# A graph network kernel: weighted one-hot windows and one weight difference made by GpSimd instead of VectorE

## The chip, the cores and the metric

One Trainium2 chip, one core. The metric is the device time of the kernel in microseconds (us), the median of several executions; less is better. A profile is one further execution with the hardware profiler on; its times are counted from the start of its span.

## The reference

The inputs are 625 nodes with 256 features, 10625 edges in order of their destination (`src`, `dst`), a weight for each edge, and the weight matrices. Cut to what matters:

```python
def edge_conv(x, src, dst, W, b):
    m = concat([x[dst], x[src] - x[dst]]) @ W + b
    return segment_sum(m, dst, 625) / maximum(count(dst), 1)

h = relu(layernorm(x));  xs = [h]
for W, b in ((W0, b0), (W1, b1), (W2, b2)):
    h = relu(edge_conv(h, src, dst, W, b));  xs.append(h)
x = x + concat(xs) @ Wf + bf
h = relu(layernorm(x))
agg = segment_sum(edge_weight * (h @ W4)[dst], src)
x = x + relu(batchnorm(agg + bias) * gamma + beta)
```

Since `[x_i, x_j - x_i] @ [Wa; Wb]` is `x_i @ (Wa - Wb) + x_j @ Wb`, each layer has own terms with the difference of the two halves of its weights, and neighbour terms that a matrix of edge counts sums up.

## The kernel before, in words

The edges are never gathered. The kernel builds two dense 625x625 matrices, the edge counts and the summed edge weights, and then works with matrix products alone.

**The build.** The edges are cut into 85 tiles of 125. Tile t gives a one-hot of its sources (`src_hot`, 125 edges by 626 nodes in f16), and a narrow one-hot of its destinations: as the edges are sorted by destination, those of a tile fall into a window of 28 nodes. Windows are made for a class of 17 tiles at once (`PER` = 17, classes 0 to 4). `plain_window(c)` (L569 to 572) compares the window's ids with the edges' destinations and writes `dst_hot[:, c, 0]`, 125x504 f16. `weighted_window(c)` (L574 to 579) multiplies that by the high and the low part of the edge weights and writes `dst_hot[:, c, 1:3]`, 125x1008 f16. TensorE multiplies source one-hot by the three kinds of destination one-hot (L1276, 505 products), block of 125 destinations by block (r = 0 to 4). Block 0 takes tiles 0 to 18 and block 1 tiles 15 to 35, each for five column groups s; from block 1 on, the tiles of a block come in two halves, and only the first column group of a half waits for tiles that are new.

**Who makes what.** VectorE makes the source tiles in order (L583, `source_tile`), one `tensor_scalar` each, 77 of the 85. ScalarE makes eight of them (`SCALAR_TILES`) by two activations each. The order of VectorE's other work in the build is written out by hand in a loop over t (from L622): at tile 13 the vectors, at the last tile but one of each class (t % 17 == 15) the next class's plain and weighted window, at tiles 30, 38 and 42 the low part of u (L596), which wait for ScalarE's high part and so for TensorE, at tile 33 `difference(0)` (L586 to 590), which subtracts the halves of layer 0's weights in `raw[0]` in place, and at tile 62 the test of the flag. There are 36 slots for source tiles (`RING`): tile t waits until TensorE has finished with tile t - 36.

**What waits for it.** Before the first tile of a class TensorE waits for that class's weighted window (`weighted_windows_ready`, L1264 to 1265). Between the blocks it does other work: within block 0 the transposes of h and the neighbour terms of blocks 0 and 1, behind it those of the other blocks (L1189), and behind block 1 layer 0's own terms (L1200, `own_terms_0`, which waits for `w_diff`). SP reloads `raw[0]` once the own terms are done.

**GpSimd** makes constants in the first 4 us. Then it waits for all 77 source tiles of VectorE (`pool.wait_ge(src_hot_vector, 77)`), sums parts of the weights (L487) and makes low parts of weight matrices (L481) in the later stages.

**Behind the build** come the three layers. VectorE forms the reciprocals of the counts (L659, L661) right behind its last source tile, and then for each quarter of a layer `pre = sum * inv_count` (L742, the sum in PSUM) and `pre = pre + own` (L746, all in SBUF).

Of the kernel before, what the change touches and what calls it, by code (L numbers as in the profile page):

```python
# [34 lines left out]
ALU = mybir.AluOpType  # L35
# [7 lines left out]
KF = D // P  # L43
LAYERS = 3
NB = 5
BLK = NODES // NB
EP = 125
TILES = EDGES // EP
PER = TILES // NB
# [14 lines left out]
FULL = 112  # L64
SCALAR_EARLY, SCALAR_NEXT, SCALAR_LATER = (0, 4), (22, 27), {0: (34, 38), 1: (52,), 2: (71,)}
SCALAR_TILES = SCALAR_EARLY + SCALAR_NEXT + sum(SCALAR_LATER.values(), ())
VECS_AT, DIFF_AT = 13, 33
U_AT = (30, 38, 42)
FLAG_AT = 62

# [84 lines left out]
def gnn_kernel(nc, x, src, dst, edge_weight, W0, b0, W1, b1, W2, b2, Wf, bf, W4, b4, gamma, beta, out):  # L155
    with ExitStack() as ctx:
# [3 lines left out]
        def sem(name):  # L160
            return ctx.enter_context(nc.semaphore(name))
# [140 lines left out]
        rel_ready = sem("rel_ready")  # L302
        window_ready = sem("window_ready")
        weighted_windows_ready = sem("weighted_windows_ready")
        dev_ready = sem("dev_ready")
        flag_ready = sem("flag_ready")
        src_hot_vector = sem("src_hot_vector")
# [146 lines left out]
        @block.gpsimd  # L454
        def _(pool):
            step = Steps(pool, pool_steps)

            step.add(pool.memset(ident[:, :], 0.0))
            step.wait()
            pool.affine_select(out=ident[:, :], in_=ident[:, :], compare_op=ALU.not_equal, fill=1.0,  # L460
                               base=0, pattern=[[-1, P]], channel_multiplier=1).then_inc(ident_ready, 1)
            pool.iota(base_id[:, :, :].rearrange("p c (a b) -> p c a b", b=3),
                      [[BLK, NB], [22, 6], [7, 3]], base=-MARGIN, channel_multiplier=0,
                      allow_small_or_imprecise_dtypes=True).then_inc(constants_ready, 1)
            pool.wait_ge(ident_ready, 1)
            pool.tensor_copy(ident_h[:, :], ident[0:TILES, 0:TILES]).then_inc(constants_ready, 1)
            step.add(pool.iota(node_id[:, :], [[1, OH]], base=0, channel_multiplier=0,
                               allow_small_or_imprecise_dtypes=True))
            step.wait()
            pool.tensor_copy(pair_id[:, :, :],  # L470
                             node_id[:, 0:WINDOW].unsqueeze(2).to_broadcast([EP, WINDOW, 2])).then_inc(constants_ready, 1)
            pool.wait_ge(padding_ready, 1)
            pool.affine_select(out=degree_f[:, :], in_=degree_f[:, :], compare_op=ALU.not_equal, fill=1.0,
                               base=-DEGREE, pattern=[[0, P]], channel_multiplier=1).then_inc(constants_ready, 1)
            pool.affine_select(out=edgeless_row[:, :], in_=edgeless_row[:, :], compare_op=ALU.not_equal, fill=1.0,
                               base=-EDGELESS, pattern=[[0, 1]], channel_multiplier=1).then_inc(constants_ready, 1)

            def low_part(n_hi, lo, source, hi):

                pool.wait_ge(w_hi, n_hi)  # L480
                pool.tensor_tensor(lo, source, hi.bitcast(F32), ALU.subtract).then_inc(w_lo_pool, 1)  # L481

            def sum_weights(r):

                pool.wait_ge(parts_copied, NB * (r + 1))
                part = parts[:, r, :, :, :]
                pool.tensor_tensor(part[:, :, 0, :], part[:, :, 0, :], part[:, :, 1, :],  # L487
                                   ALU.add).then_inc(weights_summed, 1)

            pool.wait_ge(src_hot_vector, TILES - len(SCALAR_TILES))  # L490
            for r in EARLY_SUMS:
                sum_weights(r)
            low_part(HI_WF1, wf1[1][:, :, :], raw[0][:, 0:KF, :], wf1[0][:, :, :])
            pool.wait_ge(block_built, NB * NB)
            pool.memset(weights_hi[:, :, NODES:NODES_E].bitcast(F32), 0.0)
            pool.memset(weights_lo[:, :, NODES:NODES_E].bitcast(F32), 0.0).then_inc(weights_padded, 1)
            pool.wait_ge(u_lo_ready, NB + 1)
            low_part(HI_WB2, wb[2][1][:, :, :], raw[2][:, KF:2 * KF, :], wb[2][0][:, :, :])
            low_part(HI_WD2, wd[2][1][:, :, :], raw[2][:, 0:KF, :], wd[2][0][:, :, :])
            sum_weights(2)  # L500
            low_part(HI_WF23, wf23_lo[:, :, :], raw[1][:, :, :], wf23_hi[:, :, :])
            pool.wait_ge(u_lo_ready, 2 * NB + 1)
            sum_weights(3)
            sum_weights(4)
            low_part(HI_W4, w4[1][:, :, :], raw[2][:, 0:KF, :], w4[0][:, :, :])

        @block.vector
        def _(dve):
# [77 lines left out]
            def difference(l):  # L586

                r = raw[l]
                dve.wait_ge(raw_loaded[l], 16)
                dve.tensor_tensor(r[:, 0:KF, :], r[:, 0:KF, :], r[:, KF:2 * KF, :], ALU.subtract).then_inc(w_diff, 1)  # L590
# [31 lines left out]
            for t in range(TILES):  # L622
                if t == VECS_AT:
                    groups.wait_filled(dve, "vecs")
                    dve.wait_ge(constants_ready, 4)
                    dve.tensor_copy(vecs[:, :], groups.bank["vecs"][:, 0:6 * KF]).then_inc(vecs_ready, 1)
                    dve.tensor_copy(degree_r[:, :], degree_f[:, :]).then_inc(degree_ready, 1)
                if t % PER == PER - 2 and t // PER + 1 < NB:
                    plain_window(t // PER + 1)
                    weighted_window(t // PER + 1)  # L630
                if t in U_AT:
                    blocks = U0_BLOCKS[U_AT.index(t)]
                    low_rows(("u", 0, blocks[0]), blocks[0], blocks[-1] + 1, len(blocks))
                if t == DIFF_AT:
                    difference(0)
                if t == FLAG_AT:
                    groups.wait_filled(dve, "dev")
                    step.add(dve.tensor_reduce(worst[:, :], groups.bank["dev"][0:1, 0:EP], AX.X, ALU.max))
                    step.wait()
                    dve.tensor_scalar(flag[:, :], worst[:, :], 0.5, None, ALU.is_gt).then_inc(flag_ready, 1)  # L640
                if t >= RING:
                    dve.wait_ge(*last_half(t - RING))
                source_tile(t)
# [262 lines left out]
        def _(act):  # L906
# [20 lines left out]
            def high_part(o, i):  # L927
                copy(o, i).then_inc(w_hi, 1)
# [108 lines left out]
            for l in range(LAYERS):  # L1037
                if l >= 1:
                    for b in range(NB):
                        high_rows(("u", l, b), b)  # L1040
                    own_terms(l)
                    if l == 1:
                        act.wait_ge(weights_padded, 1)
                    for i in WT_TURNS[l]:
                        turned_high(i)
                if l == 1:
                    act.wait_ge(raw_loaded[1], 32)
                    high_part(wf23_hi[:, :, :], raw[1][:, :, :])
                for q, (f, h) in enumerate(QUADS):
                    a, e = HALVES[h]  # L1050
                    act.wait_ge(z_ready, 4 * l + q + 1)
                    nc.scalar.activation(h_hi[l + 1][:, f, a:e], pre_t[:, f, a:e], ACT.Relu).then_inc(h_hi_ready, 1)  # L1052
                if l == 0:
                    act.wait_ge(w_diff, 2)
                    high_part(wd[1][0][:, :, :], raw[1][:, 0:KF, :])
                    act.wait_ge(w_diff, 3)
                    high_part(wd[2][0][:, :, :], raw[2][:, 0:KF, :])
                if l == 1:
                    act.wait_ge(raw_loaded[2], 32)
                    high_part(w4[0][:, :, :], raw[2][:, 0:KF, :])  # L1060
# [61 lines left out]
        def _(pe):  # L1122
# [69 lines left out]

            def own_terms_0():

                pe.wait_ge(w_diff, 1)
                for q, (f, h) in enumerate(QUADS):
                    a, e = HALVES[h]
                    o = fill(("own", 0, q))[:, 0:e - a]
                    for k in range(KF):
                        ins = pe.matmul(o, raw[0][:, k, P * f:P * (f + 1)], h0_t[:, k, a:e],  # L1200
                                        start=(k == 0), stop=(k == KF - 1))
                    ins.then_inc(filled, 1)
# [55 lines left out]
            def wait_tile(t):  # L1258
                made[t in SCALAR_TILES] += 1
                if t in SCALAR_TILES:  # L1260
                    pe.wait_ge(src_hot_scalar, made[1])
                else:
                    pe.wait_ge(src_hot_vector, made[0])
                if t % PER == 0:  # L1264
                    pe.wait_ge(weighted_windows_ready, t // PER + 1)

            seen = 0
            for r in range(NB):
# [234 lines left out]
```

## Time and profile before

| | |
|---|---|
| median of 3 runs | 111.92 us (111.76 to 112.2) |
| the profiled execution | 111.94 us |
| its span | 110.1 us |
| TensorE matmul busy | 100.2 us, 91% |
| TensorE weight load busy | 92.3 us, 84% |
| VectorE busy | 87.6 us, 80% |
| ScalarE busy | 62.5 us, 57% |
| GpSimd busy | 16.6 us, 15% |

PE is TensorE's matmul, PEld its weight load (which overlaps the matmuls), DVE is VectorE, ACT ScalarE, POOL GpSimd. A row of a timeline merges neighbouring instructions of one line and shape; its length runs from the first start to the last end. The recorded length of an instruction overlaps that of its neighbour by some 0.1 us, so what one costs an engine that is never idle is read from start to start.

### The profile page before, as it was taken

Reading aid. Unit: us, or ns where it says so; the run is one execution under the profiler, and the core shown is the slowest. Engines: PE = TensorE matmul, PEld = TensorE weight load, DVE = VectorE, ACT = ScalarE, POOL = GpSimd, SP = SyncE. Lnnn points to the kernel's source line nnn. Section 1 sums busy time; section 2 is a strip of 40 time slices with the busy share of each in tenths; the row PEclk is TensorE's granted clock in tenths of the full one; section 3 lists DMA queues with packets and bytes.
Section 4 is the critical chain, followed back from the end, with each engine's and each line's share of the span. In section 5 each row is a group of like instructions: output and inputs, shape, how many; then the busy total and the mean of one; then the engine's idle time right before and its main releaser. Section 6 shows DMA issues by size and latency. Waiting matters only on the chain.

```text
span 110.1 us, 2688 instructions
## 1 busy us (share of the span) xinstructions
PE 100.2 (91%) x1040; PEld 92.3 (84%) x1040; DVE 87.6 (80%) x259; ACT 62.5 (57%) x151; POOL 16.6 (15%) x24
## 2 busy tenths in 40 slices
PE   0299999799999999999999999999999999999950
PEld 0344998787898989989999999999999999999640
DVE  2499999999999998999933599831999989728950
ACT  1497999998797964312858135457413144332640
POOL 7200000000000076000093800390000000000000
PEclk9999999999999999999999999999999999999996
DMA  1876910000110000000143000000000000000026
GB/s 31 249 211 150 299 65 0 0 6 3 49 52 0 6 6 3 6 0 3 17 173 96 5 0 0 0 6 0 0 6 0 0 0 0 0 0 6 0 72 164
DMA packets 5401, 4.63 MB, mean 42 GB/s; under 512 B 555, under 2 KB 5386, under 8 KB 5386
## 3 DMA queue, kind: packets, MB, share of 16 engines
q1 hardware_dynamic: 4460, 3.68, 11.7%
q10 hardware_dynamic: 926, 0.75, 2.5%
q8 instruction: 10, 0.16, 0.6%
q14 instruction: 5, 0.04, 0.1%
HBM read 3.79 MB, written 0.64 MB: 40 GB/s over the span
## 4 chain that ended last, share of the span: by engine, by line
PE 61%; DVE 28%; DMA 3%; issue 3%; ACT 1%; SPq 0%; DVEq 0%; ACTq 0%
DVE src_hot L583 17%; PE bank L1377 14%; PE bank L1126 10%; PE bank L1127 10%; PE bank L1128 10%; PE bank L1276 5%; PE bank L1210 4%; DMA edge_rows_i<-in_dst_dram 3%; PE bank L1415 2%; PE bank L1355 2%; DVE dst_hot L572 2%; DVE stats L536 1%; DVE u_lo L596 1%; DVE dst_hot L579 1%; PE bank L1460 1%
## 5 line engine op out<-in xcount | busy, mean ns | idle before, releaser
L583 DVE TENSOR_SCALAR src_hot<-node_id,edge_cols 125x626 f16<-125x626 f16 x77 | 23.5, 379 | 0.0
L1276 PEld LDWEIGHTS bank<-dst_hot,src_hot 125*128 125x128 f16 x505 | 19.0, 98 | 3.1 <-DVE src_hot L583 1.7
L1276 PE MATMUL bank<-dst_hot,src_hot 125*128 125x84 f16 (+6 forms) x505 | 20.4, 195 | 1.2 <-DVE src_hot L583 0.9
L1377 PE MATMUL bank<-counts,u_lo 125*128 125x312 f32 (+3 forms) x60 | 16.7, 309 | 0.0
L1052 ACT ACTIVATE h_hi<-pre 128x312 fp32r<-128x312 f32 (+1 forms) x12 | 5.6, 466 | 16.9 <-DVE pre L746 16.9
L1377 PE MATMUL bank<-counts,u_hi 125*128 125x312 f32 (+3 forms) x48 | 14.0, 307 | 0.0
L487 POOL TENSOR_TENSOR parts<-parts 125x625 f32<-125x625 f32 x5 | 6.4, 1299 | 42.9 <-DVE src_hot L583 35.8
L1377 PEld LDWEIGHTS bank<-counts,u_lo 125*128 125x128 f32 (+1 forms) x60 | 11.0, 189 | 0.0
L992 ACT ACTIVATE parts<-bank 125x250 f32<-125x250 f32 x25 | 10.2, 409 | 0.0
L762 DVE TENSOR_TENSOR weights_lo<-bank,weights_hi 125x500 fp32r<-125x500 f32 (+1 forms) x7 | 3.9, 616 | 7.1 <-ACT weights_hi L911 7.1
L1377 PEld LDWEIGHTS bank<-counts,u_hi 125*128 125x128 f32 (+1 forms) x48 | 9.1, 189 | 0.0
L953 ACT ACTIVATE own<-bank,vecs 128x312 f32<-128x312 f32 (+1 forms) x12 | 6.3, 524 | 4.1 <-PE bank L1128 3.1
L1126 PE MATMUL bank<-wf_hi,h_hi 128*125 128x256 f32 x30 | 8.4, 281 | 0.0
L1127 PE MATMUL bank<-wf_hi,h_lo 128*125 128x256 f32 x30 | 8.4, 281 | 0.0
L1128 PE MATMUL bank<-wf_lo,h_hi 128*125 128x256 f32 x30 | 8.4, 281 | 0.0
L746 DVE TENSOR_TENSOR pre<-pre,own 128x312 f32<-128x312 f32 (+1 forms) x12 | 6.7, 557 | 0.4
L742 DVE TENSOR_TENSOR pre<-bank,inv_count 128x312 f32<-128x312 f32 (+1 forms) x12 | 5.7, 478 | 1.3 <-PE bank L1377 1.3
L911 ACT ACTIVATE counts<-bank 125x125 fp32r<-125x125 f32 x20 | 5.8, 291 | 1.7 <-PE bank L1276 1.7
L937 ACT ACTIVATE distance<-node_id,edge_cols 125x626 f16<-125x626 f16 x8 | 6.6, 829 | 0.1
L911 ACT ACTIVATE u_hi<-bank 125x256 fp32r<-125x256 f32 (+1 forms) x13 | 5.2, 417 | 2.5 <-PE bank L1128 2.5
L1126 PE MATMUL bank<-weights_hi,u_hi 125*128 125x312 f32 (+1 forms) x20 | 6.3, 317 | 0.0
L596 DVE TENSOR_TENSOR u_lo<-bank,u_hi 125x256 fp32r<-125x256 f32 (+1 forms) x13 | 5.6, 458 | 0.9 <-ACT u_hi L911 0.9
(146 smaller groups left out, 250.9 us busy)
## 6 DMA issues: line engine op xcount, KB each, us to landing
raw<-in_L_gnn_W_dram SPq DMA_DIRECT2D x3, 512.0 KB, 7.0
x_in<-in_x_dram ACTq DMA_DIRECT2D x1, 560.0 KB
raw<-in_L_gnn_Wf_dram SPq DMA_DIRECT2D x1, 512.0 KB, 3.8
out_dram<-x_in SPq DMA_DIRECT2D x2, 168.0 KB
wf<-in_L_gnn_Wf_dram SPq DMA_DIRECT2D x1, 256.0 KB, 8.0
raw<-in_L_gnn_Wf_dram SPq DMA_DIRECT2D x1, 256.0 KB, 2.6
raw<-in_L_gnn_W_dram SPq DMA_DIRECT2D x1, 256.0 KB, 4.4
out_dram<-x_in SPq DMA_DIRECT2D x2, 112.0 KB
```

The costliest lines, as they stand in the source:

```text
L487: pool.tensor_tensor(part[:, :, 0, :], part[:, :, 0, :], part[:, :, 1, :], ALU.add).then_inc(weights_summed, 1)
L583: dve.tensor_scalar(src_hot[:, t % RING, 0:IDS], node_id[:, 0:IDS], edge_cols[:, 0, t:t + 1], None, ALU.is_equal).then_inc(src_hot_vector, 1)
L596: dve.tensor_tensor(u_lo[0:BLK, b:b + n, :], rows, u_hi[0:BLK, b:b + n, :].bitcast(F32), ALU.subtract).then_inc(u_lo_ready, n)
L746: dve.tensor_tensor(pre_t[:, f, a:e], pre_t[:, f, a:e], own[:, f, a:e], ALU.add).then_inc(z_ready, 1)
L911: copy = lambda o, i: nc.scalar.activation(o, i, ACT.Copy)
L937: nc.scalar.activation(distance[:, :], node_id[:, 0:IDS], ACT.Abs, bias=edge_cols[:, 0, t:t + 1], scale=-1.0).then_inc(distance_ready, 1)
L992: nc.scalar.activation(parts[:, r, s, :, :], built[s][0:BLK, 1:KINDS, 0:BLK], ACT.Copy, scale=1.0 / WEIGHT_SCALE).then_inc(parts_copied, 1)
L1126: pe.matmul(o, lh, rh, start=start, stop=False)
L1127: pe.matmul(o, ll, rh, start=False, stop=False)
L1128: return pe.matmul(o, lh, rl, start=False, stop=stop)
L1276: return pe.matmul(built[s][:, :, n0:n0 + n], src_hot[:, t % RING, BLK * s:BLK * s + P], dst_hot[:, c, :, j // 2, c0:c0 + n, j % 2], start ...
L1377: ins = pe.matmul(bank[KF * h + f][:, 0:e - a], u[0:n, k, P * f:P * (f + 1)], counts[0:n, k, a:e], start=False, stop=(k == NB - 1 and u is ...
```

## The change

GpSimd gets a new stretch ahead of its wait for the source tiles. As soon as VectorE has made plain window c (c = 1 to 4), GpSimd makes the weighted one; after class 1 it also makes the difference of layer 0's weights. VectorE makes the plain window of the next class at tile 5 of a class instead of tile 15, twelve tiles ahead of its first use, and no longer makes weighted windows 1 to 4 or the difference of layer 0. TensorE waits for the two new semaphores. Window 0 stays on VectorE whole, and so do the differences of layers 1 and 2.

```diff
-VECS_AT, DIFF_AT = 13, 33
+VECS_AT, PLAIN_AT = 13, 5
...
+        weighted_windows_pool = sem("weighted_windows_pool")
+        w_diff_pool = sem("w_diff_pool")
...
         @block.gpsimd
...
+            pool.wait_ge(weight_parts_ready, 2)
+            for c in range(1, NB):
+                pool.wait_ge(window_ready, c + 1)
+                shape = [EP, KINDS - 1, PAIRS, WINDOW, 2]
+                part = weight_parts[:, c].rearrange("p k (a b) -> p k a b", b=2).unsqueeze(3).to_broadcast(shape)
+                plain = dst_hot[:, c, 0].unsqueeze(1).to_broadcast(shape)
+                pool.tensor_tensor(dst_hot[:, c, 1:KINDS], plain, part, ALU.mult).then_inc(weighted_windows_pool, 1)
+                if c == 1:
+                    pool.wait_ge(raw_loaded[0], 16)
+                    pool.tensor_tensor(raw[0][:, 0:KF, :], raw[0][:, 0:KF, :], raw[0][:, KF:2 * KF, :],
+                                       ALU.subtract).then_inc(w_diff_pool, 1)
             pool.wait_ge(src_hot_vector, TILES - len(SCALAR_TILES))
...
         @block.vector
...
-                if t % PER == PER - 2 and t // PER + 1 < NB:
+                if t % PER == PLAIN_AT and t // PER + 1 < NB:
                     plain_window(t // PER + 1)
-                    weighted_window(t // PER + 1)
                 if t in U_AT:
                     blocks = U0_BLOCKS[U_AT.index(t)]
                     low_rows(("u", 0, blocks[0]), blocks[0], blocks[-1] + 1, len(blocks))
-                if t == DIFF_AT:
-                    difference(0)
...
         @block.scalar
...
+                    act.wait_ge(w_diff, 1)
+                    high_part(wd[1][0][:, :, :], raw[1][:, 0:KF, :])
                     act.wait_ge(w_diff, 2)
-                    high_part(wd[1][0][:, :, :], raw[1][:, 0:KF, :])
-                    act.wait_ge(w_diff, 3)
                     high_part(wd[2][0][:, :, :], raw[2][:, 0:KF, :])
...
         @block.tensor
...
-                pe.wait_ge(w_diff, 1)
+                pe.wait_ge(w_diff_pool, 1)
...
-                if t % PER == 0:
-                    pe.wait_ge(weighted_windows_ready, t // PER + 1)
+                if t == 0:
+                    pe.wait_ge(weighted_windows_ready, 1)
+                elif t % PER == 0:
+                    pe.wait_ge(weighted_windows_pool, t // PER)
```

## Rows read from the trace of the kernel before

**Rows 1.** The page: busy us (share of the span) xinstructions of each engine

```profile
PE 100.2 (91%) x1040; PEld 92.3 (84%) x1040; DVE 87.6 (80%) x259; ACT 62.5 (57%) x151; POOL 16.6 (15%) x24
```

**Rows 2.** The chain that ended last, 9 to 42 us: start us, us, what

```profile
9.70 3.30 DVE src_hot L583 x11
...
33.86 1.27 DVE src_hot L583 x4
...
35.17 3.05 PE bank L1276 x81
...
39.27 1.33 PE bank L1276 x41
```

**Rows 3.** Timeline of TensorE's weight loads in the build: start us, us, engine, line, what

```profile
22.12 1.98 PEld L1276 LDWEIGHTS bank<-dst_hot,src_hot 125*128 125x128 f16 x47 [0.80 <-DVE src_hot L583]
...
34.88 0.10 PEld L1276 LDWEIGHTS bank<-dst_hot,src_hot 125*128 125x128 f16 x1 [0.20 <-DVE src_hot L583]
35.17 2.92 PEld L1276 LDWEIGHTS bank<-dst_hot,src_hot 125*128 125x128 f16 x81 [0.20 <-DVE src_hot L583]
...
38.82 1.67 PEld L1276 LDWEIGHTS bank<-dst_hot,src_hot 125*128 125x128 f16 x50 [0.20 <-DVE src_hot L583]
```

**Rows 4.** Timeline of VectorE in the build

```profile
5.54 0.41 DVE L572 TENSOR_TENSOR dst_hot<-pair_id,rel 125x504 f16<-125x504 f16 x1
5.87 0.33 DVE L604 CAST weight_parts<-bank 125x170 f16<-125x170 f32 x1
...
13.71 0.41 DVE L572 TENSOR_TENSOR dst_hot<-pair_id,rel 125x504 f16<-125x504 f16 x1
14.16 0.68 DVE L579 TENSOR_TENSOR dst_hot<-dst_hot,weight_parts 125x1008 f16<-125x1008 f16 x1
14.76 3.89 DVE L583 TENSOR_SCALAR src_hot<-node_id,edge_cols 125x626 f16<-125x626 f16 x13
...
21.09 0.68 DVE L590 TENSOR_TENSOR raw<-raw 128x512 f32<-128x512 f32 x1
21.69 1.26 DVE L583 TENSOR_SCALAR src_hot<-node_id,edge_cols 125x626 f16<-125x626 f16 x4
22.86 0.68 DVE L596 TENSOR_TENSOR u_lo<-bank,u_hi 125x512 fp32r<-125x512 f32 x1
```

**Rows 5.** GpSimd's groups of instructions by shape: busy us, mean ns | idle before

```profile
L487 POOL TENSOR_TENSOR parts<-parts 125x625 f32<-125x625 f32 x5 | 6.4, 1299 | 42.9 <-DVE src_hot L583 35.8 <-DVE u_lo L596 7.2
L481 POOL TENSOR_TENSOR wf_lo<-raw,wf_hi 128x1024 fp32r<-128x1024 f32 x1 | 2.4, 2407 | 2.3 <-ACT wf_hi L911 2.3
...
L481 POOL TENSOR_TENSOR wf_lo<-raw,wf_hi 128x512 fp32r<-128x512 f32 x1 | 1.3, 1300 | 0.0
```

**Rows 6.** Timeline of TensorE's matmuls in block 0 and behind it

```profile
14.83 1.86 PE L1276 MATMUL bank<-dst_hot,src_hot 125*128 125x60 f16 x50
16.55 2.83 PE L1189 MATMUL bank<-raw,h_t 128*125 128x256 f32 x12
```

**Rows 7.** Timeline of GpSimd in layer 1

```profile
60.95 2.41 POOL L481 TENSOR_TENSOR wf_lo<-raw,wf_hi 128x1024 fp32r<-128x1024 f32 x1 [2.26 <-ACT wf_hi L911]
```

**Rows 8.** Timeline of VectorE in layer 1

```profile
61.83 0.48 DVE L742 TENSOR_TENSOR pre<-bank,inv_count 128x312 f32<-128x312 f32 x1 [1.08 <-PE bank L1377]
62.34 1.35 DVE L746 TENSOR_TENSOR pre<-pre,own 128x312 f32<-128x312 f32 x1
...
64.12 0.48 DVE L746 TENSOR_TENSOR pre<-pre,own 128x312 f32<-128x312 f32 x1
```

**Rows 9.** Timeline of VectorE behind the build

```profile
41.60 1.72 DVE L661 RECIPROCAL inv_count<-inv_count 128x250 f32<-128x250 f32 x1
43.55 0.48 DVE L742 TENSOR_TENSOR pre<-bank,inv_count 128x312 f32<-128x312 f32 x1 [0.24 <-PE bank L1377]
```

## The prediction

> **What bounds the kernel now.** I read the page's busy table first, then the chain that ended last, then each engine's timeline over the build, and last GpSimd's instructions in the later stages.
>
> Over the whole span TensorE is busy 91%, VectorE 80%, GpSimd 15% [rows 1]. That average hides two regimes, and the chain of waits separates them. From 9.70 us to about 35.1 us the chain is almost only VectorE, above all its source tiles at L583; from 35.17 us on it is TensorE [rows 2]. So in the build (9.7 to 40.6 us), where one-hots are made and multiplied, VectorE sets the pace, but barely. TensorE's weight loads sat idle behind L583 for 0.80 us before 22.12 and for 0.20 us each before 34.88, 35.17 and 38.82 us [rows 3]. That is 1.4 us, and with the one short load between 34.88 and 35.17 some 1.6 us: this is all that a faster VectorE can give back. The other direction isn't bounded in that way. The last 41 products (L1276) start at 39.27 us in the chain, right behind VectorE's last tiles [rows 2], so a VectorE that comes later by one microsecond makes the end of the build later by one.
>
> **What leaves VectorE.** A plain window alone takes 0.33 us from its start to the next start (5.54 to 5.87). A plain one with its weighted one takes 1.05 us (13.71 to 14.76) [rows 4]. So a weighted window costs 0.71 us, with the wait on its own predecessor; there are four, 2.84 us. The difference at L590 takes 0.60 us (21.09 to 21.69) [rows 4]. Sum: 3.44 us less work for VectorE. The plain windows only move, from tile 15 to tile 5 of each class, at the same price. The change adds no DMA. The reload of `raw[0]` on SP still waits for layer 0's own terms, and moves with them; waits renumbered on ScalarE (w_diff 1 and 2) keep their meaning.
>
> **What GpSimd gets.** Four products of 125x1008 f16 and one subtraction of 128x512 f32. The trace has no GpSimd product in f16, so I bound it. 128x1024 f32 took 2.41 us, 128x512 took 1.30 us, 125x625 took 1.30 us [rows 5]. The nearest in size is the 1024 row: 1.11 us for 512 further elements is 2.17 ns each, so 1008 elements are 2.38 us, which I take. Upper end: 1008 at the rate of the 512 row, 2.56 us. Lower end: VectorE did 1008 f16 in the time of 512 f32 (0.68 us both) [rows 4]; if GpSimd won as much by 16 bits, 1.30 us. The subtraction is 1.30 us. In all 4 x 2.38 + 1.30 = 10.8 us of GpSimd, which is idle in the build.
>
 By the traced durations (2.41 us for 1024 is 2.35 ns each) it is a little more, and the sum goes by those.
>
> Is GpSimd in time by itself? Plain window 1 now stands behind tile 4, so VectorE finishes it near 10.9 us; GpSimd could have weighted it by about 13.4 us and the difference by about 14.7 us. TensorE takes tiles 9 to 18 in the 50 products from 14.83 us [rows 6], so tile 17 begins near 16.3 us, and the own terms only after 24 us. The later windows have some 5 us each. Alone, GpSimd is never late.
>
> **The term that decides: what VectorE does meanwhile.** In layer 1 GpSimd ran one instruction from 60.95 to 63.36 us [rows 7]. VectorE's L742, one of whose inputs is in PSUM, ran beside it in its usual 0.48 us. L746, whose two inputs both lie in SBUF, began at 62.34 and took 1.35 us; its twin at 64.12, with GpSimd idle, has 0.48 [rows 8]. So it stood still for 0.87 us, until about 0.15 us before GpSimd's recorded end: a GpSimd product can hold VectorE off for what is left of it.
>
> Are the source tiles of the build of that kind? They read one SBUF tensor. But 13 of them take 3.89 us, 0.30 us each for 626 elements. The two-input windows take 0.60 us for 1008 and 0.33 us for 504, so 0.53 ns for each further element; at that rate 626 elements alone are 0.33 us, without any fixed part [rows 4]. The tiles are faster than VectorE can be over what a two-input instruction leaves it for each tensor, so they use more of its way into SBUF than L742 does. I take it that they are held off as L746 was.
>
> The Trainium skill, page "SBUF — State Buffer", section "Who interferes with whom", says that a `tensor_scalar` in a two-port mode and an instruction with two SBUF inputs contend with GpSimd, and that the one that comes second blocks for the whole instruction. The row of L746 agrees (0.87 us); for tiles no run here shows it yet.
>
> **The sum.** Each GpSimd instruction then costs VectorE its duration less 0.15 us: 4 x 2.23 + 1.15 = 10.1 us. Less the 3.44 us removed, VectorE ends the build 6.6 us later. In stages: by 15 us it has lost 2.23 + 1.15 and saved 0.71, so tile 18 comes 2.7 us later and TensorE stalls there, ahead of the u terms at 16.55 [rows 6]; by the second half of block 1 a second window has been added and another window and the difference saved, making about +3.5 us at the place where it stalls 0.80 us now [rows 3]; windows 3 and 4 add 1.5 us each. All of it lies ahead of the last tile, for which TensorE waits already (0.20 us before 38.82), so nothing hides it. What follows has no cover either: the reciprocal that ends with the build's work ends at 43.32 and the next instruction begins at 43.55 [rows 9], and it moves along with the tiles. Behind that TensorE is the chain and unchanged.
>
> The profiled execution had 111.94 us (span 110.1 and 1.8 around it), and the median of the runs is 111.92, so they are one number. 111.94 + 6.6 = **118.6 us**. Low end of this case: a window at 1.30 us, 5 x 1.15 - 3.44 = +2.3, 114.3. High end: 2.56 us and nothing given back early, 11.5 - 3.4 = +8.1, 120.0.
>
> **Rivals.**
>
> *VectorE keeps its way in.* VectorE's tiles follow one another without idle time, and a trace in which GpSimd came first can't show who wins when VectorE is first. If GpSimd must wait for a pause, the first pause is tile 38, where VectorE waits for u rows of blocks 2 and 3, which TensorE makes only after tiles 17 and 18. VectorE is there at 22.86 - 2 x 0.71 - 0.60 = 20.84 us [rows 4], GpSimd is done at 23.2, and TensorE, due at 16.3, is 6.9 us late; windows 3 and 4 can repeat it in part. 119 to 124 us. For it: no idle on VectorE. Against: each instruction's end is a chance to change over. The same section of the SBUF page says that issue order decides who blocks, which leaves this open.
>
> *They share.* The tiles fall to the pace of a one-way instruction, 0.33 us and the fixed part of 0.07 us that the windows show (0.60 - 1008 x 0.53 ns), 0.40 instead of 0.30 us. Over 10.8 us that loses 2.7 us against 3.44 saved, and little is left: 111.4 to 112.3, no change.
>
> *No contention (the other side).* If the tiles don't meet GpSimd at all, as L742 didn't [rows 8], VectorE is 3.44 us ahead, TensorE's stalls of 1.6 us go, and TensorE becomes the bound of the build: 110.3 us, faster. The sign turns where GpSimd's five instructions together hold VectorE for less than 3.44 us of their 10.8. For it: L583 reads a single SBUF tensor. Against: its speed, and L746. The SBUF page's rule that an instruction with at most one SBUF input outside the two-port modes doesn't contend would give this time, if the tiles were outside them.
>
> **How the numbers follow.** A measurement of this kernel can tell about 0.5% (0.6 us) from no change. Held off as L746: 0.62. VectorE keeps its way in: 0.15. Something between, held off for part of each instruction, 112.6 to 114.4: 0.03. Shared, no change: 0.05. No contention, faster: 0.15. Slower is 0.62 + 0.15 + 0.03 = 0.80. The range leaves out the last two: it begins at 114.3, the low end of the likeliest case, and ends at 122.5, inside the second case's range. The likeliest case alone has 114.3 to 120.0.
>
> **What would show it.** In the changed profile: GpSimd with four products of about 2.4 us and one of 1.3 between 11 and 40 us; next to each, one L583 of 2 us or more instead of 0.38, while the others keep 0.38; VectorE's busy time about 6 us up although its work is less; TensorE's stalls behind L583 several times the 1.4 us of [rows 3], the first large one before tile 17 or 18; the last tile near 46 us instead of 39. A GpSimd span far over 2.5 us with tiles at 0.38 would speak for the first rival; all tiles at 0.38 and a last one near 36 us would make the forecast wrong in sign; tiles near 0.5 us mean sharing.

## The result, and the profile after

The change made the kernel slower: 116.27 us (116.18 to 116.64, 4 runs) against 111.96 us, a ratio of 1.038 (95% interval 1.036 to 1.041), so 4.3 us lost. The prediction had 118.6 us with a range of 114.3 to 122.5 and gave slower a chance of 0.8. The profiled execution took 116.18 us, its span is 114.1 us, 4.0 more than before; the other 0.2 us lie outside the span (2.1 us of the time instead of 1.8). The lines of code have moved: the source tiles are L596 (L583 before), the plain windows L585, the products of the build L1288 (L1276), and GpSimd's new product and difference are L498 and L501.

The page of the changed kernel, busy time by engine, which answers to [rows 1]:

```profile
PE 100.9 (88%) x1040; PEld 92.2 (81%) x1040; DVE 91.8 (80%) x254; ACT 62.4 (55%) x151; POOL 25.6 (22%) x29
```

VectorE has five instructions less and is busy for 4.2 us more (87.6 before). Its groups of instructions by shape show where: 77 tiles now have 30.8 us of recorded time instead of 23.5 (the first row is from before).

```profile
L583 DVE TENSOR_SCALAR src_hot<-node_id,edge_cols 125x626 f16<-125x626 f16 x77 | 23.5, 379 | 0.0
L596 DVE TENSOR_SCALAR src_hot<-node_id,edge_cols 125x626 f16<-125x626 f16 x77 | 30.8, 471 | 0.0
```

The mean of 471 ns mixes two kinds. The timeline of GpSimd in the build:

```profile
11.16 1.88 POOL L498 TENSOR_TENSOR dst_hot<-dst_hot,weight_parts 125x1008 f16<-125x1008 f16 x1 [7.62 <-DVE dst_hot L585]
13.00 1.34 POOL L501 TENSOR_TENSOR raw<-raw 128x512 f32<-128x512 f32 x1
19.24 1.95 POOL L498 TENSOR_TENSOR dst_hot<-dst_hot,weight_parts 125x1008 f16<-125x1008 f16 x1 [4.91 <-DVE dst_hot L585]
26.20 1.95 POOL L498 TENSOR_TENSOR dst_hot<-dst_hot,weight_parts 125x1008 f16<-125x1008 f16 x1 [5.01 <-DVE dst_hot L585]
33.16 1.96 POOL L498 TENSOR_TENSOR dst_hot<-dst_hot,weight_parts 125x1008 f16<-125x1008 f16 x1 [5.01 <-DVE dst_hot L585]
```

And VectorE's timeline in the same stretches, with the two single tiles of the first (from narrower windows of it), and the end of the build:

```profile
10.59 0.42 DVE L585 TENSOR_TENSOR dst_hot<-pair_id,rel 125x504 f16<-125x504 f16 x1
...
11.21 2.00 DVE L596 TENSOR_SCALAR src_hot<-node_id,edge_cols 125x626 f16<-125x626 f16 x1
...
13.14 1.38 DVE L596 TENSOR_SCALAR src_hot<-node_id,edge_cols 125x626 f16<-125x626 f16 x1
...
25.71 0.42 DVE L585 TENSOR_TENSOR dst_hot<-pair_id,rel 125x504 f16<-125x504 f16 x1
26.03 2.59 DVE L596 TENSOR_SCALAR src_hot<-node_id,edge_cols 125x626 f16<-125x626 f16 x3
...
36.40 0.27 DVE L648 TENSOR_REDUCE worst<-bank 1x1 f32<-1x125 f32 x1
...
36.77 6.52 DVE L596 TENSOR_SCALAR src_hot<-node_id,edge_cols 125x626 f16<-125x626 f16 x22
43.21 0.40 DVE L669 TENSOR_SCALAR inv_count<-bank 128x250 f32<-128x250 f32 x1
```

The same two instructions, the flag's test and the one behind the last tile, before:

```profile
31.28 0.27 DVE L638 TENSOR_REDUCE worst<-bank 1x1 f32<-1x125 f32 x1
...
39.13 0.41 DVE L659 TENSOR_SCALAR inv_count<-bank 128x250 f32<-128x250 f32 x1
```

The tile that starts just behind GpSimd's product takes 2.00 us instead of 0.37, and ends 0.17 us behind it (13.21 against 13.04). The next starts at 13.14 and takes 1.38 us, until GpSimd's difference is over. Each of the later products holds one tile in the same way (26.03: three tiles in 2.59 us, against 3 x 0.29 + 0.08). All other tiles keep their pace, as the 22 from 36.77 on do. VectorE's build work ends at 43.21 us; before, L659 followed its last tile at 39.13. That is +4.08 us.

In the chain that ended last the tiles grow from 17% to 25% of the span, and VectorE now leads the chain until 43.00 us (35.17 before, [rows 2]). TensorE's weight loads sat idle behind the tiles for 3.4 us in all, against 1.7 before, and they show two waits that I had not predicted; of the stalls:

```profile
13.27 0.20 PEld L1288 LDWEIGHTS bank<-dst_hot,src_hot 125*128 125x128 f16 x5 [1.20 <-DVE src_hot L596]
14.57 0.20 PEld L1288 LDWEIGHTS bank<-dst_hot,src_hot 125*128 125x128 f16 x5 [1.11 <-DVE src_hot L596]
...
29.01 1.88 PEld L1210 LDWEIGHTS bank<-h_t,raw 128*128 128x128 f32 x8 [0.86 <-DVE u_lo L609]
...
36.95 0.19 PEld L1261 LDWEIGHTS bank<-counts,degree_r 128*128 128x128 f32 x1 [1.81 <-issue]
```

and the last of them among the matmuls, with its releaser:

```profile
36.98 0.35 PE L1261 MATMUL bank<-counts,degree_r 128*128 128x250 f32 x1 [1.75 <-DVE flag L650]
```

The third is ahead of the second half of layer 0's own terms, which waits for VectorE's low part of u. The last is a wait that I hadn't looked for: the counts need bank 6, which is free only when VectorE has tested the flag at tile 62. VectorE comes to it at 36.40 us instead of 31.28, and TensorE stands still ahead of 36.95 for 1.8 us. Experiments e5 and e8 below ask what that is worth.

### The profile page after: what moved, and what is told of

Same layout as the page of the kernel before. It is cut to its first block, busy times and chain, and to the rows that moved or that the text cites. A ratio compares the mean times of both kernels' runs of the same rounds, so it can differ in the third digit from the quotient of the medians.

```text
span 114.1 us, 2688 instructions
## 1 busy us (share of the span) xinstructions
PE 100.9 (88%) x1040; PEld 92.2 (81%) x1040; DVE 91.8 (80%) x254; ACT 62.4 (55%) x151; POOL 25.6 (22%) x29
## 4 chain that ended last, share of the span: by engine, by line
PE 55%; DVE 32%; DMA 4%; issue 2%; ACT 1%; ACTq 1%; DVEq 0%
DVE src_hot L596 25%; PE bank L1389 14%; PE bank L1136 10%; PE bank L1137 10%; PE bank L1138 10%; DMA x_in<-in_x_dram 4%; PE bank L1220 4%; PE bank L1427 2%; PE bank L1367 2%; DVE stats L549 2%; PE bank L1288 1%; DVE u_lo L609 1%; DVE dst_hot L585 1%; PE bank L1472 1%; ACT pre L1103 1%
## 5 line engine op out<-in xcount | busy, mean ns | idle before, releaser
L596 DVE TENSOR_SCALAR src_hot<-node_id,edge_cols 125x626 f16<-125x626 f16 x77 | 30.8, 471 | 0.0
L1288 PEld LDWEIGHTS bank<-dst_hot,src_hot 125*128 125x128 f16 x505 | 18.9, 98 | 4.9 <-DVE src_hot L596 3.4
L1288 PE MATMUL bank<-dst_hot,src_hot 125*128 125x84 f16 (+6 forms) x505 | 20.4, 195 | 2.5 <-DVE src_hot L596 2.2
L498 POOL TENSOR_TENSOR dst_hot<-dst_hot,weight_parts 125x1008 f16<-125x1008 f16 x4 | 7.7, 1932 | 22.5 <-DVE dst_hot L585 22.5
```

Source lines behind the costliest of these rows:

```text
L498: pool.tensor_tensor(dst_hot[:, c, 1:KINDS], plain, part, ALU.mult).then_inc(weighted_windows_pool, 1)
L596: dve.tensor_scalar(src_hot[:, t % RING, 0:IDS], node_id[:, 0:IDS], edge_cols[:, 0, t:t + 1], None, ALU.is_equal).then_inc(src_hot_vector, 1)
L1288: return pe.matmul(built[s][:, :, n0:n0 + n], src_hot[:, t % RING, BLK * s:BLK * s + P], dst_hot[:, c, :, j // 2, c0:c0 + n, j % 2], start ...
```

## The experiments

Ten kernels ran, in three steps. The theory: a GpSimd instruction and a fast source tile can't touch SBUF at once, and VectorE, which bounds the build, pays for it. The rivals: the moved plain windows, late weighted windows, and the stall at the flag.

**e1, the early plain windows alone.** From the kernel before:

```diff
-                if t % PER == PER - 2 and t // PER + 1 < NB:
+                if t % PER == 5 and t // PER + 1 < NB:
                     plain_window(t // PER + 1)
+                if t % PER == PER - 2 and t // PER + 1 < NB:
                     weighted_window(t // PER + 1)
```

> The kernel before with one part of the change alone: VectorE makes the plain windows at tile 5 of a class, and everything else stays on VectorE where it was. Held-off theory: the move costs nothing by itself, 111.7 to 112.3 us, no tile longer than 0.4 us. A theory in which the early plain windows delay the tiles that TensorE waits for in block 0 would give up to 4 x 0.33 = 1.3 us more, 113.3.

Measured: 112.03 us against 112.07, ratio 0.999 (0.998 to 1.001); no tile over 0.39 us. The move is free.

**e2, the windows on GpSimd, the difference on VectorE.** From the changed kernel, with the waits for the difference set back:

```diff
-                if c == 1:
-                    pool.wait_ge(raw_loaded[0], 16)
-                    pool.tensor_tensor(raw[0][:, 0:KF, :], ..., ALU.subtract).then_inc(w_diff_pool, 1)
...
+                if t == 33:
+                    difference(0)
```

> The changed kernel with the difference of layer 0's weights back on VectorE at tile 33. Held-off theory: GpSimd's difference held VectorE for 1.0 us and its own cost on VectorE is 0.60 us, so this is 0.4 us faster than the changed kernel, 115.8 to 115.9 us, and VectorE still stands still for 1.6 us beside each of four windows. If instead it were the raw total of VectorE's work that counts and GpSimd didn't matter, it would be 0.6 us slower, 116.9.

Measured: 117.0 to 117.1 us in three executions and 115.71 in the fourth, ratio 1.040 (1.033 to 1.046). Neither theory had that spread. The trace splits it. VectorE did what was expected of the held-off theory: its tiles ended at 42.80 us, 0.41 earlier than in the changed kernel. But TensorE ended the build later. Behind the pause at the flag its granted clock was 0.5, the lower of its two levels, 1.2 GHz. The busy times of e2 by stretches (length, then PE, PEld, DVE, ACT, POOL with their instructions, then PEclk and the share and rate of DMA):

```profile
36.00:38.00 2.00, 1.41 (x22) 1.41 (x23) 1.97 (x9) 1.33 (x2) 0.00 (x0) 0.72 0.00 0
38.00:40.00 2.00, 2.00 (x36) 2.00 (x35) 2.00 (x8) 0.00 (x0) 0.00 (x0) 0.50 0.00 0
```

The same stretches of the changed kernel, with a pause just as long:

```profile
36.00:38.00 2.00, 1.02 (x25) 1.01 (x26) 1.97 (x9) 1.71 (x4) 0.00 (x0) 1.00 0.00 0
38.00:40.00 2.00, 2.00 (x61) 2.00 (x58) 2.00 (x9) 0.45 (x3) 0.00 (x0) 1.00 0.00 0
```

Between 38 and 40 us 36 products against 61. The first sums of layer 0 began 1.49 us behind the last tile in the changed kernel (44.70 and 43.21) and 2.85 us in e2 (45.65 and 42.80): 1.36 us, the size of the spread. The profiled execution is one of the three long ones; the fourth wasn't profiled, but its mean granted clock over the whole run is 1.00 where theirs is 0.98 to 0.99, and its 115.71 us are about what the held-off theory expected (115.8 to 115.9). So the clock differs between executions of one kernel.

**e3, each of GpSimd's products twice.**

```diff
+                step.add(pool.tensor_tensor(dst_hot[:, c, 1:KINDS], plain, part, ALU.mult))
+                step.wait()
                 pool.tensor_tensor(dst_hot[:, c, 1:KINDS], plain, part, ALU.mult).then_inc(...)
```

> The changed kernel with each of GpSimd's four products made twice (the second gives the same values again, behind the first). Held-off theory: each further product of 1.94 us holds VectorE for another 1.5 to 1.9 us, in all 6 to 7.6 us: 122.3 to 123.9 us. If TensorE waited for the late weighted windows rather than for tiles, only those would count whose window comes later than TensorE's need: window 1 would be ready at about 15.1 us, ahead of tile 17, and the time would stay within 1 us of 116.3.

Measured: 124.25 us, ratio 1.109 (1.106 to 1.112). VectorE's build ended at 49.92 us, 6.71 later than in the changed kernel, 1.68 us for each further product. The time is 0.35 us above the expected range. The rest is the clock again, at 0.5 from 46 to 48 us: the sums begin 2.67 us behind the last tile. The end of a run of tiles in e3, where the second product holds one as the first does:

```profile
29.44 4.24 DVE L598 TENSOR_SCALAR src_hot<-node_id,edge_cols 125x626 f16<-125x626 f16 x3
```

Three tiles in 4.24 us: one for each product, and one as usual. A late window isn't the cause: behind the first products, TensorE's long waits in the build are for tiles (1.64 us ahead of 15.31), for the low part of u (2.02 ahead of 34.07) and for the flag (1.82 ahead of 43.70), all from VectorE, and none is for a window.

**e4, tiles in a slower form.** The 22 tiles beside GpSimd's work compare the same ids, read from a copy with gaps, which GpSimd makes at 3.5 us:

```diff
+        gap_id = sb("gap_id", [EP, IDS // 2, 4], F16)
...
+                    ids = gap_id[:, :, 0:2] if t in ONE_WAY else node_id[:, 0:IDS]
-                    dve.tensor_scalar(src_hot[:, t % RING, 0:IDS], node_id[:, 0:IDS], ...)
+                    dve.tensor_scalar(src_hot[:, t % RING, 0:IDS], ids, ...)
```

> The changed kernel with another form for the 22 source tiles that VectorE makes beside GpSimd's instructions: the same comparison with the same result, but read from a copy of the ids that is laid out in pairs with gaps, so that its outermost dimension is 313 long while the output's is 626. Theory (the tiles are held off because the fast form uses both of VectorE's ways into SBUF): such a tile falls back to the pace of two elements at a time over one way, 0.40 to 0.45 us from start to start instead of 0.30, and isn't held off; 22 x 0.11 = 2.4 us instead of 7.5 us lost, 116.3 - 5.1 = 111.2 us, with none of these tiles over 0.6 us. Rival (GpSimd holds off any instruction of VectorE that reads or writes SBUF in the build): the holds of 1.6 us stay, 116.3 to 118.7 us. The trace tells whether the other form is taken at all: if the tiles stay at 0.30 us from start to start where GpSimd is idle, it isn't.

Measured: 112.31 us against 112.07, ratio 1.001 (0.999 to 1.003). VectorE's timeline beside GpSimd's first product and the difference (11.58 to 14.69 us there):

```profile
11.34 0.38 DVE L603 TENSOR_SCALAR src_hot<-node_id,edge_cols 125x626 f16<-125x626 f16 x1
11.63 3.21 DVE L603 TENSOR_SCALAR src_hot<-gap_id,edge_cols 125x626 f16<-125x626 f16 x7
14.76 0.17 DVE L646 COPY vecs<-bank 128x12 f32<-128x12 f32 x1
```

Seven tiles in 3.13 us from start to start, 0.447 each instead of 0.29, and none held; GpSimd's products take 1.88 and 1.95 us as in the changed kernel. The size of one term was off: a tile in the slow form costs 0.15 us more and not 0.11, so 22 of them cost 3.4 us, just what GpSimd takes off VectorE. That decides the cause. With GpSimd's work in the build the same and only the form of 22 tiles changed, some 4.0 of the 4.3 us are gone. By the span all of it is: 110.0 to 110.5 us, as before, against 114.1 to 114.5; the 0.2 us outside the span stay. The Trainium skill, page "SBUF — State Buffer", section "Who interferes with whom", says that one-input instructions outside the two-port modes don't contend with GpSimd, and the trace agrees (0 held of 22); that the form with gaps is outside those modes is inferred from its pace, 0.447 us instead of 0.29.

**e7, GpSimd writes only.** e1 with four instructions of GpSimd that read nothing:

```diff
+            for c in range(1, NB):
+                pool.wait_ge(window_ready, c + 1)
+                step.add(pool.iota(scratch[:, :, :], [[0, 3], [1, 628]], base=0, channel_multiplier=0, ...))
```

> e1 (all windows on VectorE, plain ones early) with a GpSimd instruction beside the tiles that writes SBUF and reads none: four iotas of 3 x 628 f16 into memory that nobody reads, each behind a plain window. By the early iota of 628, 0.66 us, one takes about 2 us. Held-off theory in its wide form (the fast tiles write over both ways too): each iota holds a tile for 1.6 us as a product does, 112.0 + 6.5 = 118.5 us. Narrow form (only reads collide): 112.0 us and no tile over 0.4 us.

Measured: a median of 118.12 us, ratio 1.053 (1.051 to 1.055); one execution of 338.69 us is unexplained, and the ratio leaves it out. An iota of 1.78 to 1.84 us holds a tile, too:

```profile
26.81 2.45 DVE L589 TENSOR_SCALAR src_hot<-node_id,edge_cols 125x626 f16<-125x626 f16 x3
29.18 0.41 DVE L602 TENSOR_TENSOR u_lo<-bank,u_hi 125x256 fp32r<-125x256 f32 x1
```

2.37 us for three tiles, 1.5 more than 3 x 0.29. So what collides isn't GpSimd's reads alone, and it needs neither a product nor the window's memory.

**e5, the flag's test at tile 54 in e2.** `FLAG_AT = 62` becomes 54.

> e2 (the changed kernel with the difference on VectorE) with one edit: the test of the flag at tile 54 instead of 62. In e2's profile TensorE waited 1.75 us for that test (bank 6, ahead of the counts at 36.59 us), and then ran from about 37 to 41 us at a granted clock of 0.5, so that it and not VectorE ended the build. Theory (the pause let the clock fall): without the pause no stretch at 0.5 in the build, and the time is what e2 was expected to have, 115.7 to 115.9 us instead of 117.0. Rival (the clock falls in this kernel in any case, or the windows alone cost more than with the difference): it stays at 117.0.

Measured: 121.92 us in all four executions, ratio 1.088 (1.086 to 1.089). Both theories missed it, and the trace shows what my first rival was about, VectorE keeping its way in. GpSimd's four products in e5:

```profile
11.00 1.88 POOL L498 TENSOR_TENSOR dst_hot<-dst_hot,weight_parts 125x1008 f16<-125x1008 f16 x1 [7.46 <-DVE dst_hot L581]
18.07 1.95 POOL L498 TENSOR_TENSOR dst_hot<-dst_hot,weight_parts 125x1008 f16<-125x1008 f16 x1 [5.19 <-DVE dst_hot L581]
25.62 1.95 POOL L498 TENSOR_TENSOR dst_hot<-dst_hot,weight_parts 125x1008 f16<-125x1008 f16 x1 [5.61 <-DVE dst_hot L581]
32.96 9.86 POOL L498 TENSOR_TENSOR dst_hot<-dst_hot,weight_parts 125x1008 f16<-125x1008 f16 x1 [5.38 <-DVE dst_hot L581]
```

VectorE's timeline there:

```profile
32.81 8.28 DVE L592 TENSOR_SCALAR src_hot<-node_id,edge_cols 125x626 f16<-125x626 f16 x28
```

TensorE's matmuls there:

```profile
42.97 4.99 PE L1286 MATMUL bank<-dst_hot,src_hot 125*128 125x30 f16 x82 [5.96 <-POOL dst_hot L498]
```

The fourth product lasted 9.86 us. Beside it VectorE made 28 tiles on end at 0.29 us, none held, and ended them at 41.0 us; GpSimd's product ended 1.8 us later, which is about its own length. The reading that fits is that it got little or nothing done while the tiles ran. TensorE waited 5.96 us for that window, and behind the wait its clock was 0.5 from 43 to 48 us, so that the clock has a part in the lost time too. With the test at tile 62 there are six tiles behind the plain window of class 4 and then a `tensor_reduce`; with the test moved ahead, nothing but tiles.

**e8, the same edit in the changed kernel.** 

> The changed kernel with the test of the flag at tile 54 instead of 62, and nothing else. Its profile shows the same pause of 1.75 us on TensorE (before 36.98 us) but a clock of 1.00 behind it, and VectorE's tiles end the build. Held-off theory: the pause is made up before the last tile, so this is the changed kernel's 116.3 us within 0.3 us. Rival (the pause is part of the 4.3 us lost): up to 1.8 us faster, 114.5.

Measured: 116.31, 116.54, 121.99 and 122.37 us, a median of 119.26. The profiled one is the first: no stall at the flag any more (TensorE's weight loads have no idle time before the counts), and yet the time of the changed kernel. So the pause of 1.8 us is made up before the last tile, and no part of the 4.3 us. The two long ones are as long as e5 is; neither was profiled, so that their fourth product was as late as e5's is inferred from their time.

**e9 and e10, a pause of VectorE's.** e5 and e8 with

```diff
+                if t == 58:
+                    dve.tensor_reduce(pause[:, :], dev[:, 1, :], AX.X, ALU.max)
```

> e5 with one small VectorE instruction more: at tile 58, two tiles behind the plain window of class 4, a tensor_reduce over 85 elements whose result nobody reads (0.2 to 0.3 us, one SBUF input). In e5 GpSimd's fourth product took 9.86 us: it began at 32.96 us, just behind the start of a tile, and ended 1.8 us after the last of 28 tiles that ran at 0.29 us each, none held; all four executions took 121.9 us. Theory (who is first keeps the way, and GpSimd gets in at VectorE's first instruction that isn't a two-way one): GpSimd starts its work at the pause at the latest, takes 2 to 3 us in all, TensorE doesn't wait for the window, and the time is 115.7 to 116.3 us. Rival (the fourth product is slow for another reason, as its place or what TensorE or ScalarE do then): it stays at 9 to 10 us, and the time near 122.

> e8 (the changed kernel with the flag's test at tile 54) with the same small instruction at tile 58. e8's four executions took 116.3, 116.5, 122.0 and 122.4 us. Theory: the two long ones are those in which GpSimd's fourth product lost against 28 tiles on end; with the pause all executions take 116.2 to 116.7 us. Rival: the spread stays.

Measured: e9 115.92 to 116.39 us (median 116.09, ratio 1.037, 1.035 to 1.039), e10 116.29 to 116.62 (median 116.32, ratio 1.040, 1.038 to 1.043). The 122s are gone in all eight executions. But the profiles show GpSimd first in both, ahead of the pause, so that none shows it getting in at the pause. The fourth product in e9, and VectorE's tiles beside it:

```profile
33.49 1.96 POOL L499 TENSOR_TENSOR dst_hot<-dst_hot,weight_parts 125x1008 f16<-125x1008 f16 x1 [5.38 <-DVE dst_hot L582]
```

```profile
33.34 2.29 DVE L593 TENSOR_SCALAR src_hot<-node_id,edge_cols 125x626 f16<-125x626 f16 x2
35.55 0.23 DVE L651 TENSOR_REDUCE pause<-dev 125x1 f32<-125x85 f32 x1
```

What the runs show is that with it no execution was long; that the pause bounds the wait is the reading that fits. e9 also answers what e5 was made to ask: it is e2 without the stall at the flag and with one small instruction more, its clock is 1.00 throughout the build, and its 116.1 us are 0.9 below e2's 117.0.

**e6, one window, where no tile is near.** From the kernel before, class 1 alone:

```diff
             plain_window(0)
+            plain_window(1)
...
                 if t % PER == PER - 2 and t // PER + 1 < NB:
-                    plain_window(t // PER + 1)
-                    weighted_window(t // PER + 1)
+                    if t >= PER:
+                        plain_window(t // PER + 1)
+                        weighted_window(t // PER + 1)
...
+            pool.wait_ge(vector_steps, 2)
+            pool.wait_ge(weight_parts_ready, 1)
+            pool.wait_ge(window_ready, 2)
...
+            pool.tensor_tensor(dst_hot[:, 1, 1:KINDS], plain, part, ALU.mult).then_inc(weighted_windows_pool, 1)
```

> The kernel before with GpSimd making only the weighted window of class 1, and at another time: VectorE makes that class's plain window right behind that of class 0, and GpSimd weights it from about 6.8 to 8.8 us, while VectorE takes the statistics of x (one input in SBUF each) and no source tile exists yet. The rest is as before. Held-off theory: nothing of VectorE is held, its two-input window of class 0 comes just behind; 0.7 us less VectorE work in a build that it bounds, of which TensorE's 1.4 to 1.6 us of stalls can take all: 111.2 to 111.6 us. Rival (any GpSimd product holds VectorE, statistics too): 1.6 us lost against 0.7 saved, 112.9. Rival (TensorE or the later start of the first tiles bounds it): 111.9 to 112.2.

Measured: 111.55 us against 112.11, ratio 0.995 (0.994 to 0.997): a gain of 0.56 us, small but clear of the noise. GpSimd works from 6.86 to 8.74 us; VectorE's five statistics of x beside it take what they take before, 1.72 us, and its build ends at 38.37 us, 0.76 before 39.13, against 0.71 expected:

```profile
6.86 1.88 POOL L497 TENSOR_TENSOR dst_hot<-dst_hot,weight_parts 125x1008 f16<-125x1008 f16 x1 [3.31 <-DVE dev L617]
```

```profile
7.05 1.72 DVE L544 BATCH_NORM_STATS2 stats<-x_in 125x6 f32<-125x256 f32 x5
...
9.11 0.65 DVE L587 TENSOR_TENSOR dst_hot<-dst_hot,weight_parts 125x1008 f16<-125x1008 f16 x1
...
38.37 0.40 DVE L669 TENSOR_SCALAR inv_count<-bank 128x250 f32<-128x250 f32 x1
```

## Why the prediction was right, and where it was off

**What bounds the kernel** was read rightly. VectorE's end of the build moved by +4.08 us and the span by +4.0; in e6 it moved by -0.76 and the time by -0.56. e1 shows that the order of the windows is worth nothing.

**The term that decides** was right in kind. I had one row for it, L746 held for 0.87 us in layer 1 [rows 8], and an argument from speed that the tiles are of the same kind. The changed kernel shows five tiles held, and e4 shows that it is the tiles' fast form that makes them so. Which side wins when VectorE is first stayed a guess in the forecast.

**Its price was too high**, by 2.5 us on VectorE (+6.6 against +4.08), and that is all of the 2.3 us between forecast and result, as 0.2 us more lie outside the span. The term that was mis-sized is "the nearest in size is the 1024 row ... 1008 elements are 2.38 us". The f16 product took 1.88 to 1.96 us, between my row and the lower end of 1.30. And "its duration less 0.15 us" should have been less 0.32 (1.95 - 1.63). With what was measured, 4 x 1.63 held by the products and 1.01 by the difference (1.38 - 0.37) are 7.5 us, less the 3.44 us removed +4.1, and VectorE showed +4.08. The removed work was sized rightly, then. The Trainium skill, page "GPSIMD Engine Reference", section 3.1, would have given an estimated 2.18 us by its 2.6 cycles per element, nearer than my row but still too much; its measured example is in f32, and here the f16 product took about 1.9 ns per element, 2.3 cycles at the page's 1.2 GHz.

**The stages.** TensorE's first large stalls came not at tile 17 or 18 but right behind the hold, at 13.27 and 14.57 us: I had placed them where TensorE catches up with VectorE for good, but it takes the early tiles one by one as they come. At 17.15 us its matmuls began the ten tiles that began at 14.83 before [rows 6], 2.3 us late where I had 2.7 for tile 18. The second half of block 1 came 2.25 us late (its weight loads at 24.37 instead of 22.12), where I had 3.5. And the stalls behind the tiles only doubled, from 1.7 to 3.4 us, where I had named several times 1.4 as a sign; the rest of TensorE's delay came as the waits for the low part of u and for the flag (0.86 and 1.8 us). The wait for the flag's test I had missed: the test stands behind VectorE's stretches of tiles, and so moves with them. In the changed kernel it cost nothing (e8, 116.3), but by the clock it can cost 1.2 to 1.4 us (e3, e2). The forecast has no term for it, and that it came out at nothing is luck.

**The rivals.** No contention: refuted by the five held tiles; it would need tiles that are fast and yet not held beside a GpSimd instruction that gets on, and the only fast tiles that ran on beside one, e5's 28, stand against a product that took 9.86 us. Shared: refuted, since one tile takes about the whole length of each GpSimd instruction, and all others have their usual pace, none the 0.40 us of that rival. VectorE keeps its way in: I took it for another outcome of the same kernel, with a chance of 0.15. By e5 it is the same mechanism from the other side, and by e8's two times it can come out differently in executions of one kernel. The changed kernel's five meetings in the profile all went to GpSimd. e5's fourth went to VectorE, and cost 5.8 us more than e9. In the changed kernel a lost meeting should be short, though no profile shows one, as each of its stretches of tiles behind a plain window is broken after 3 to 8 tiles by an instruction of another kind.

**What stays open.** Why e5 was long in every execution, and so by its profile lost the fourth meeting, and e8 in two of four. The recorded starts don't tell them apart: GpSimd's product begins 0.15 us behind the start of a tile in e5, and 0.15 to 0.16 us behind it in e8's profile and in e9, too, where it won. Also open is why the clock fell behind the pause in one profile (e2) and not in another (the changed kernel), and in three of e2's four executions by their mean clocks.

## What to carry to other kernels

Before work is given to an idle GpSimd, look at what VectorE does at that time, not at how busy GpSimd is: an instruction of VectorE that runs at its fastest over SBUF stands still for nearly the whole of a GpSimd instruction, so that moving 0.71 us of VectorE's work cost it 1.63. Place such work beside VectorE's slower one-input instructions, as e6 did, and price it from a row of the same type, or give the range both ends. And never let a GpSimd instruction that someone waits for meet a long unbroken row of fast VectorE instructions: it may not get in before their end, as in e5.

## What the runs showed of the hardware that I had not expected

GpSimd and VectorE's fast tiles exclude each other in both directions, and in e5 the loser waited as long as the other's row lasted. When GpSimd was first, one tile was held for 1.63 us by a product of 1.95 us; between two GpSimd instructions VectorE got in with that one tile (it ended at 13.21 us in the changed kernel, and the next, from 13.14, was held by the difference). When VectorE was first, GpSimd didn't get in between any of 28 tiles, 8.2 us (e5).

An iota of GpSimd, which has no input, holds a tile as a product does (1.5 us of 1.8, e7).

The same `tensor_scalar` over 626 f16 elements takes 0.29 us from start to start when its input is contiguous, and 0.447 us when its input is laid out in 313 pairs with gaps; in the second form it keeps that pace beside GpSimd (e4).

TensorE's granted clock was 0.5 for some 3 us behind a pause of 1.8 us in e2's profile, and 1.00 behind a pause of the same length in the changed kernel's; e2's fourth execution has a mean clock of 1.00, so that it isn't fixed by the kernel.
